# SyncE's order of issues around the scratch round trip in the attention layers

## The reference

```python
x = _layernorm(x + _L0_gnn_ref(x, adj, ...))            # graph attention layer
# three times, with weights of their own:
q = _heads(x @ Wq + bq); k = _heads(x @ Wk + bk); v = _heads(x @ Wv + bv)
scores = jnp.einsum('bhqd,bhkd->bhqk', q, k) / np.sqrt(64)
probs = jax.nn.softmax(scores + jnp.where(adj, 0.0, NEG)[:, None], axis=-1)
ctx = jnp.einsum('bhqk,bhkd->bhqd', probs, v)
x = _layernorm(x + ctx.reshape(32, 256, 384) @ Wf + bf)
```

## Time and profile before

| | us |
|---|---|
| three runs | 3033.63, 3040.04, 3040.24 |
| median | 3040.04 |
| the profiled execution | 3031.44 |
| its span | 3029.7 |
| TensorE busy in the span | 2752.4 |
| VectorE | 2437.9 |
| ScalarE | 2362.9 |
| GpSimd | 1805.6 |

### The profile page before, as it was taken

One profiled execution on the slowest core, in us unless ns is written; L12 is line 12 of the kernel. 1 busy time (PEld: TensorE's weight loads), 2 busy tenths in 40 slices (PEclk: granted clock), 3 DMA queues, 4 the chain that ended last, 5 costly groups with the idle time before them and its releaser, 6 DMA issues. The chain is left out here.

```text
span 3029.7 us, 66563 instructions
## 1 busy us (share of the span) xinstructions
PE 2752.4 (91%) x20128; PEld 2457.8 (81%) x20128; DVE 2437.9 (80%) x7209; ACT 2362.9 (78%) x6600; POOL 1805.6 (60%) x1550
## 2 busy tenths in 40 slices
PE   8999999999988899899898898898989998989886
PEld 7888888888877788788787788888888887888875
DVE  6999999999877778778787777787777787877775
ACT  7999999999976677777776677677777776777764
POOL 3777766666655656655555556656555555555554
PEclk9999999999999999999999999999999999999997
DMA  2111111111157766766776766767767667677674
GB/s 89 35 35 36 35 35 36 35 35 35 42 176 232 209 211 217 218 209 213 218 220 210 234 209 216 212 215 216 219 204 217 216 210 218 211 219 221 208 216 164
DMA packets 383585, 500.40 MB, mean 165 GB/s; under 512 B 58112, under 2 KB 345728, under 8 KB 382848
## 3 DMA queue, kind: packets, MB, share of 16 engines
q1 hardware_dynamic: 383232, 496.16, 53.3%
HBM read 219.24 MB, written 201.33 MB: 139 GB/s over the span
## 5 line engine op out<-in xcount | busy, mean ns | idle before, releaser
L557 POOL TENSOR_TENSOR probs<-probs,recs 128x1024 f32<-128x1024 f32 x288 | 545.8, 1895 | 794.4 <-DVE recs L1048 794.4
L764 ACT ACTIVATE split<-pj,bc 128x256 fp32r<-128x256 f32 x576 | 241.5, 471 | 522.3 <-issue 398.2
L779 ACT ACTIVATE probs<-logits,nmax 128x256 f32<-128x256 f32 x1152 | 575.5, 504 | 65.3 <-DVE turned_sb L1056 59.0
L1056 DVE STREAM_TRANSPOSE turned_sb<-probs 128x512 f32<-128x512 f32 x576 | 605.0, 1090 | 9.3 <-DMA turned<-turned_sb 6.1
L1026 DVE SCALAR_TENSOR_TENSOR split<-pj,bc,split 128x256 fp32r<-128x256 f32 x576 | 248.3, 473 | 321.4 <-ACT split L764 318.8
L772 ACT ACTIVATE stack<-split 64x768 fp32r<-64x768 f32 x576 | 485.8, 843 | 3.4
L76 PE MATMUL pj<-xt_hi,w_lo 128*128 128x256 f32 x1728 | 483.3, 280 | 3.1 <-DVE xt_lo L1020 3.1
L78 PE MATMUL pj<-xt_hi,w_hi 128*128 128x256 f32 x1728 | 482.4, 279 | 0.0
L77 PE MATMUL pj<-xt_lo,w_hi 128*128 128x256 f32 x1728 | 482.3, 279 | 0.0
L1035 DVE CUSTOM_DVE_ANT_0 logits<-s,mask 128x256 f32<-128x256 f32 x1152 | 438.6, 419 | 1.4
L1452 PE MATMUL pt<-pt_copy,v 128*64 128x256 f32 x1536 | 220.3, 409 | 195.9 <-issue 193.8
(11 more groups left out here) (118 smaller groups left out, 7590.1 us busy)
## 6 DMA issues: line engine op xcount, KB each, us to landing
turned<-turned_sb SPq DMA_DIRECT2D x288, 512.0 KB, 5.2
pt_copy<-turned SPq DMA_DIRECT2D x288, 512.0 KB, 4.5
stack<-split SPq DMA_DIRECT2D x576, 128.0 KB, 4.4
y<-out SPq DMA_DIRECT2D x128, 384.0 KB, 4.9
x<-y SPq DMA_DIRECT2D x96, 384.0 KB, 4.7
x<-x SPq DMA_DIRECT2D x32, 384.0 KB, 3.1
adj<-adj SPq DMA_DIRECT2D x128, 64.0 KB, 4.5
w_whole<-att_w SPq DMA_DIRECT2D x3, 2304.0 KB, 10.9
```

The source lines that it names most:

```text
L557: pool.tensor_tensor(probs[:, heads, :, :].rearrange("p h t n -> p (h t) n"), probs[:, heads, :, :].rearrange("p h t n -> p (h t) n"), rec ...
L779: last = act.activation(probs[:, (HEADS * u + h) % 4, t, :], logits[:, h % 2, t, :], ACT.Exp, scale=-1.0, bias=nmax[:, u, h, t:t + 1], acc ...
L1056: last = dve.transpose(turned_sb[b][:, :, :].rearrange("p k (z h q) -> p k z h q", z=NT, h=2 * NT)[:, :, kt], probs[:, 2 * b:2 * b + 2, :, ...
```

## The change

Only SyncE's order within a slot of the attention layers is changed. Every issue keeps its waits, its size and its addresses, and no other engine's program is touched. In the old order each fetch of `prev` 1 and 2 stands directly behind its own lay, except for the store in between. In the new order the lay of a pair is followed by two or more other issues before its fetch: lay 1, fetch 0, the two issues of move 2, lay 2, fetch 1, the two issues of move 0, fetch 2. The store (and in the very first slot the last store of the graph layer, `g_store`) stands first in the slot. `crossing` is as it was.

```diff
--- before.py
+++ after.py
@@ -380,21 +380,22 @@
                 sp.dma_start(pt_sb[:, c, :, :], turned_dram[c].rearrange("b p n -> p b n")).then_inc(fetched[c], 16)
 
             def slot(new, cur, prev, old, stored):
-                if cur:
-                    move(*cur, 2)
-                if prev:
-                    fetch(*prev, 0)
-                    lay(*prev, 1)
-                    fetch(*prev, 1)
                 if stored:
                     store(*stored)
                 elif prev == first:
                     g_store(*g_odd)
                 if prev:
+                    lay(*prev, 1)
+                    fetch(*prev, 0)
+                if cur:
+                    move(*cur, 2)
+                if prev:
                     lay(*prev, 2)
+                    fetch(*prev, 1)
+                if new:
+                    move(*new, 0)
+                if prev:
                     fetch(*prev, 2)
-                if new:
-                    move(*new, 0)
                 if cur:
                     load_again(*cur)
                     lay(*cur, 0)
```

More of the change, by code:

```diff
@@ L393, in slot @@
                 if prev:
+                    lay(*prev, 1)
[3 more added lines that the diff above has]
+                if prev:
                     lay(*prev, 2)
-                    fetch(*prev, 2)
+                    fetch(*prev, 1)
                 if new:
                     move(*new, 0)
+                if prev:
+                    fetch(*prev, 2)
                 if cur:
```

## The result

The changed kernel takes 2784.71 us (median; lowest 2779.38) beside 3040.14 us for the kernel before on the same chip. The ratio is 0.9158, with a 95% interval of 0.9129 to 0.9187: 8.4% faster. One of the changed kernel's four launches took 4315.44 us at a mean granted clock of 0.556; the ratio leaves it out, and the median of the other three, at 0.992 to 0.994, is 2779.70 us. The forecast was 2864 us with a range of 2755 to 2985. The profiled execution has a span of 2777.9 us, against 3029.7. What follows SyncE's slot function stands one line lower in the changed file, so L1452 is L1453 here, and the experiments' kernels have numbers of their own (L1456 is the same line).

A forecast was written before the change was run, and what follows sets the result against it. The last fetch, late behind SyncE's scratch waits, bounds the slot. Period 22.53 to 20.7 us over 95 periods gives 174 us, ends 2, so 2855 profiled; adding back 8.6 gives 2864 us, range 2755 to 2985.

The forecast's parts named there:

- the likeliest case: Whole kernel: forecast of 2864 us, within 2815 to 2915, a landing 0.5 us either way; chance 0.62.
- What bounds the kernel: Attention slots: the last fetch sets the slot, TensorE stalling 2.0 us on average before the last context product, 193.8 us.
- The chain of the last fetch: Slot: Q/K product ends 11.5, VectorE 13.45, fetch leaves 14.98, lands 19.5; stall near 1.1, next slot at 20.7 us.
- lay(prev,2) earlier: SyncE's slot: leaves at 8.3 at the latest, probably 7.4, instead of 10.15; landed between 12.5 and 15.0, no further delay.
- The lost clock: Attention part: a lowered stretch costs about 0.9 us of TensorE time; granted clock should rise from 0.96 to 0.99 or more.
- The store: Slot's start: held until GpSimd's layer norm ends, 0.4 us after the start; cost taken as 0, bounds 0 to +1.0 us.
- The ends: First slot's graph-layer store +2 us at most, drain's better overlap -4 us; together -2 us.
- Rival A, TensorE saturates: Slot: landing falls to 3.5 us or eviction chain shortens by 1 us; period 19.5, some 2750 us; chance 0.08.
- Rival B, crowding: Bunched issues slow transfers: last fetch lands in 5.6 us, period 21.7 to 22.1, 2955 to 3000 us; chance 0.13.
- Rivals C and E: C: store holds the queue, some 3035 us, chance 0.05; E: scratch's own pace holds, 2990 to 3040, chance 0.06.
- Rival D: Last fetch, behind the move, lands late, 6.7 us at worst; period 23.6, some 3140 us, slower; chance 0.06.
- The landing by the page: Last fetch: fixed 2.0 us plus bytes over 436 GB/s, 3.2 us for 512 KB; sum used the trace's 4.5.

The follow-up runs named there:

- The kernel without a stall: Changed kernel with fetch(prev,2) put ahead of move(new,0): 2707.32 us, ratio 0.8918 to the kernel before.
- the store's experiment: Changed kernel with the store put between move(cur,2) and lay(prev,2) instead of first in the slot: 2778.01 us, ratio 0.9149.
- the experiments behind the loads: Changed kernel with the last fetch put behind the two loads: 3126.04 us, ratio 1.0292; behind the loads and lay(cur,0): 3355.5 us, ratio 1.105.
- the delays by a wait: Changed kernel, SyncE waiting ahead of the last fetch for ScalarE's next Q/K high parts: 2872.42 us; for VectorE's turn of cur's first pair: 2965.39 us.

## Why the prediction was right, and by how much it missed

The time lies in the range, 30 us below the likeliest case's own 2815.

*What bounds the kernel.* Right. The last fetch set the slot through TensorE's stall, and the wait of SyncE behind a landing was what made the fetch late. Of the two exchanges in the old order, the one that puts the move into that wait brings 204 of the 255 us, and the one that lets the lay leave earlier brings 333.

*The chain of the last fetch.* Right as a mechanism, step by step. In the changed kernel ScalarE, VectorE and SyncE follow each other as walked; here are ScalarE and VectorE on the next Q/K chunk:

```profile
1828.35 0.84 ACT L765 ACTIVATE split<-pj,bc 128x256 fp32r<-128x256 f32 x2 [1.97 <-PE pj L78]
```

```profile
1829.22 0.88 DVE L1027 SCALAR_TENSOR_TENSOR split<-pj,bc,split 128x256 fp32r<-128x256 f32 x2 [1.07 <-ACT split L765]
```

From the end of the product (1828.15) the fetch leaves 3.50 us later; I had 3.48.

*Two terms of it were too large.* The start: the Q/K product of chunk 0 ends at 11.04, and I took 11.50 from a slot of the old kernel. That slot had a full clock, but TensorE still stood still in it: ScalarE began it with a Q/K eviction that was late, and TensorE's weight loads (PEld) stopped for 0.31 and 0.19 us among others. No row ahead of the prediction showed it:

```profile
1806.00 0.84 ACT L764 ACTIVATE split<-pj,bc 128x256 fp32r<-128x256 f32 x2 [4.72 <-issue]
```

```profile
1810.70 0.19 PEld L1439 LDWEIGHTS s<-stack 128*128 128x128 f32 x1 [0.31 <-issue]
...
1811.43 0.31 PEld L1377 LDWEIGHTS pj<-identity,x 128*128 128x128 f32 x3 [0.19 <-ACT v L753]
```

The kernel without a stall has the same 11.04, and its slot of 19.00 shows the floor that I had put at 19.5. The landing: 4.0 us where I took 4.5. With 0.1 for the last products the three make 1.05, from 20.7 to the 19.6 measured. Times 95 that is 100 us. 22 of them are lost again in slots above the typical one (19.83 against 19.6), which the sum didn't have, and 7 at the start. The 71 left are nearly the whole of the miss, 75 us between 2855 and the 2779.7 of the profiled execution. That the errors partly cancel is luck.

*lay(prev,2) earlier.* Right: it leaves 6.55 us into the slot (I had 7.4), and lands in 4.1 us, long before the fetch.

*The lost clock.* Right. I expected 0.99 or more in the attention part, and the window above has 1.00.

*The store.* I took 0, and the experiment gives 0. GpSimd's layer norm ends at 1817.71, 0.6 us after the slot's start (I had 0.4).

*The ends.* Off: I summed -2. The first sample's last fetch leaves 4.6 us later than before. In that slot SyncE stands 11.5 us for GpSimd ahead of the graph layer's last store, so that lay(prev,1) leaves at 861.12 instead of 855.93, and the move ahead of the fetch leaves only at 870.93. I had 2 us at most for this hold; which of the two makes the 4.6 isn't separated.

*Rival A, TensorE saturates.* Not in the changed kernel, which has 0.6 us of stall left, but with the fetch ahead of the move. I had tied it to a faster landing or a shorter chain of evictions; it is a matter of one more exchange, which I hadn't seen.

*Rival B, crowding.* It is there but in the wrong place for harm. fetch(prev,0), issued behind the store and a lay, now lands 5.8 us after its issue at 1819.46, against 4.5, and the median of 30 goes from 4.4 to 6.0. Nobody needs it for another 8 us or so. Part of it is the store just ahead of it: with the store further back the same fetch takes 5.0 us (median).

*Rivals C and E* fall with the time and with the store's experiment. *Rival D* didn't occur. But the experiments behind the loads show that it was priced rightly in kind: a last fetch that leaves later and lands in 5.0 us is enough to be slower than the old kernel.

*The landing by the page.* The page "DMA: Bandwidth & Descriptors" of the Trainium skill, section "Anatomy of one DMA", makes it an estimate of 3.2 us for 512 KB. The last fetch took 4.0 us, so the measurement decides: the estimate was 0.8 us too short, my 4.5 was 0.5 us too long.

## What to carry to other kernels

On a queue that issues in order, look for an issue that waits for a landing and has independent issues behind it: its price is the delay of what is queued behind it. It isn't the number of issues between a transfer and its return that counts, but that the first leaves when its data are ready and that the return has nothing ahead of it that becomes ready later. Take the length of a bound from a slot with no stalls in any engine, since a slot with a full clock may still hold small waits.

## What was not expected of the hardware

A 512 KB read took 5.2 us behind 448 KB of loads issued in the 1.2 us before it, 4.0 behind two 128 KB moves with the loads issued after it, and 3.9 behind the same moves with nothing issued in the 1.6 us after it (medians of 30 each). The first fetch of a slot took 6.0 us behind a 384 KB store and a 512 KB lay, and 5.0 behind the lay with the store moved away (medians over the slots). Why the same fetch took 4.6 us in the kernel before, with the move 0.5 us behind it, isn't settled. A read issued as soon as its data had landed isn't it: in the kernel with the fetch ahead of the move, which does the same, the median is 4.0. Whether two moves issued right behind a fetch slow it, as loads don't, no run tests.

In the slot behind the loads a stall of 3.48 us cost about 2 us beyond its own length: 0.9 in the eight products that it held up (1.98 against 1.08), and 1.1 in a stretch as far as the next Q/K product (12.15 against 11.04), whose result the next fetch depends on. The granted clock of that slot is 0.91. In the delays by a wait, with median stalls of 1.5 and 2.0 us, the attention part had 1.00 and 0.97.
